# Cross-attention and butterfly FFN on one Trainium2 core: a restaged fold, its first moves on two queues, and token rows transferred row by row

## What is computed

```python
def attn(q, k, v):                    # q = layernorm(x), k = v = context
    kv = k * v                        # along S: r = 0.9 * r + kv
    r = scan(lambda r, t: 0.9 * r + t, kv)
    return q * r
def ffn(x):
    h = x @ W_exp + b_exp             # 512 -> 2048
    h = butterfly(h, up_weights)      # 11 stages of 2x2 pairs
    h = gelu(h + up_bias)
    h = butterfly(h, down_weights)
    return h @ W_con + b_con + down_bias
x = x + attn(layernorm(x), ctx, ctx)
x = x + ffn(layernorm(x))             # x, ctx: 32 x 512 x 512
```

## Time and profile before

| | |
|---|---|
| median of 3 runs | 2850.24 us (2848.72 to 2851.96) |
| the profiled execution: its time | 2851.01 us |
| its span, first to last instruction | 2848.9 us |
| TensorE busy | 2758.7 us, 97% |
| VectorE, ScalarE, GpSimd busy | 2115.7, 1149.7, 546.7 us |
| mean granted TensorE clock | 0.983 of full |
| DMA | 541.31 MB, mean 190 GB/s; SP's queue holds 63.7% of 16 engines' span |

### The profile page before, as it was taken

How to read it: one execution, slowest core, us unless ns; L and a number is a source line. 1 busy time by engine, 2 the same in 40 slices (tenths; PEclk the granted TensorE clock), 3 DMA queues, 4 the chain that set the end, 5 groups by cost and what they waited for, 6 DMA issues and landing times.

```text
span 2848.9 us, 40884 instructions
## 1 busy us (share of the span) xinstructions
PE 2758.7 (97%) x12281; PEld 2277.6 (80%) x12281; DVE 2115.7 (74%) x3500; ACT 1149.7 (40%) x1694; POOL 546.7 (19%) x612
## 2 busy tenths in 40 slices
PE   7859999999999999999999999999999999999999
PEld 6738888888888888888888888888888888888887
DVE  5768778787777878787787878778787877778533
ACT  6554343434334343434334343333434343343432
POOL 4351212112121211212021121201112121112100
PEclk7879999999999999999999999999999999999999
DMA  7597585765758575675758567575856757585543
GB/s 191 121 339 207 161 236 149 215 187 171 223 157 235 152 220 180 178 218 163 226 154 230 168 194 208 170 217 152 247 165 188 206 163 218 155 245 165 171 155 100
DMA packets 296064, 541.31 MB, mean 190 GB/s; under 512 B 38718, under 2 KB 104414, under 8 KB 278902
## 3 DMA queue, kind: packets, MB, share of 16 engines
q1 hardware_dynamic: 290262, 536.90, 63.7%
q10 hardware_dynamic: 4848, 1.13, 0.3%
q0 software_dynamic: 688, 0.17, 0.0%
HBM read 447.89 MB, written 56.62 MB: 177 GB/s over the span
## 4 chain that ended last, share of the span: by engine, by line
PE 93%; SPq 2%; DVE 1%; DMA 1%; issue 1%; ACT 1%; POOL 1%; DVEq 0%; ACTq 0%; POOLq 0%
PE ps L1428 43%; PE ps L1446 24%; PE ps L1459 24%; SPq L458 1%; DVE xop L1056 1%; PE ps L1289 1%; DMA kv<-in_ctx_dram 1%; PE ps L1337 0%; PE ps L1339 0%; PE ps L1328 0%; SPq L422 0%; DMA w_products<-w1r 0%; SPq L428 0%; DMA w_split<-w2s_main 0%; ACT w1r L746 0%
## 5 line engine op out<-in xcount | busy, mean ns | idle before, releaser
L1428 PE MATMUL ps<-xop,w1r 128*128 128x512 f32 x5376 | 1368.7, 390 | 37.6 <-DVE xop L1056 11.9
L1428 PEld LDWEIGHTS ps<-xop,w1r 128*128 128x128 f32 x5376 | 1009.4, 188 | 255.3 <-issue 28.0
L1446 PE MATMUL ps<-w2r,ghi 128*128 128x512 f32 x2048 | 630.7, 389 | 0.0
L1459 PE MATMUL ps<-w2r,ghi 128*128 128x512 f32 x2032 | 625.7, 389 | 0.0
L833 ACT ACTIVATE st<-ps 128x512 f32<-128x512 f32 x384 | 229.4, 597 | 861.8 <-PE ps L1428 861.8
L1134 DVE TENSOR_TENSOR x<-ps,x 128x512 f32<-128x512 f32 x508 | 348.0, 685 | 278.8 <-PE ps L1459 277.9
L1446 PEld LDWEIGHTS ps<-w2r,ghi 128*128 128x128 f32 x2048 | 384.4, 188 | 80.2
L1459 PEld LDWEIGHTS ps<-w2r,ghi 128*128 128x128 f32 x2032 | 381.4, 188 | 79.4
L1157 DVE TENSOR_TENSOR glo<-g,ghi 128x512 fp32r<-128x512 f32 x510 | 381.0, 767 | 86.0 <-ACT ghi L851 85.9
L1152 DVE TENSOR_TENSOR g<-ps,st 128x512 f32<-128x512 f32 x384 | 262.8, 684 | 241.1 <-PE ps L1428 234.5
L837 ACT ACTIVATE g<-g,gelu_bias 128x512 f32<-128x512 f32 x384 | 275.4, 717 | 381.1 <-DVE g L1152 381.1
(11 more groups left out here) (140 smaller groups left out, 1818.1 us busy)
## 6 DMA issues: line engine op xcount, KB each, us to landing
w1r<-w_products SPq DMA_DIRECT2D x889, 256.0 KB, 3.3
w2r<-w_split SPq DMA_DIRECT2D x128, 1024.0 KB, 4.9
x<-in_x_dram SPq DMA_DIRECT2D x128, 256.0 KB, 6.6
raw<-kv SPq DMA_DIRECT2D x512, 64.0 KB, 2.1
out_dram<-x SPq DMA_DIRECT2D x124, 256.0 KB, 3.8
kv<-in_ctx_dram SPq DMA_DIRECT2D x64, 256.0 KB, 6.1
raw<-in_ctx_dram SPq DMA_DIRECT2D x64, 256.0 KB, 4.8
w_split<-w2s_main SPq DMA_DIRECT2D x10, 512.0 KB, 6.0
```

Source lines behind the costliest of these rows:

```text
L1428: last = nc.tensor.matmul(bank[:, :], w1r[:, slot, w, c * P:(c + 1) * P], xop[:, XPOS[m], v, c, :], start=(opens and i == 0), stop=(i == l ...
L1446: last = nc.tensor.matmul(ps_ya[j][:, :], g[:, p % 2, q, j * P:(j + 1) * P], w2r[:, p % 2, kk, w, :], start=(p == 0 and kk == 0 and i == 0 ...
L1459: last = nc.tensor.matmul(ps_yb[:, :], g[:, p % 2, q, j * P:(j + 1) * P], w2r[:, p % 2, kk, w, :], start=(kk == 0 and i == 0), stop=(kk == ...
```

## The change

- **Token rows.** `token_rows` is arranged `t j g i d`; each load and store of a step takes row j of all 128 partitions at once instead of all four rows of 32 partitions. So does the end: the last step's rows go out in four transfers, two on SP and two on ScalarE's queue, instead of sixteen, and the first half's as each is ready.
- **Split parts of the first product** are staged in two spaces by turns: even n in `xop` (positions 4 and 6), odd n in `w1r`, each with its own semaphores; `stmp` gets two sets, so that `weight_sums(n)` waits for n - 2's use.
- **Split parts of the second** go into 10 slots: six lie in blocks of `W1f` that are used up, four in `xop`.
- **Moves.** The first super-block's 32 moves are halved between SP and GpSimd's queue (`first_moves`); both wait for `low_matrix_ready`.
- **Order.** `weight_sums` runs ahead of the bias steps and `token_sums` is cut in two; w_con's upper part is loaded first; `coefs` of the down weights are split earlier; in VectorE's program the scan goes ahead of the statistics, two copies of `high_dn` go to ScalarE, and the first split parts go ahead of the second `normalise`. The copies of `WT` are shared out more evenly.

```diff
-        return a.rearrange("b s d -> (b s) d").rearrange("(g t j i) d -> g t i j d", g=G, t=T, j=J, i=Q)
+        return a.rearrange("b s d -> (b s) d").rearrange("(g t j i) d -> t j g i d", g=G, t=T, j=J, i=Q)
...
             def load_tokens(dst, h, rows, t, loaded):
-                for g in range(G):
-                    sp.dma_start(dst[Q * g:Q * g + Q, J * h:J * h + J, :], rows[g, t]).then_inc(loaded, NX)
+                for j in range(J):
+                    sp.dma_start(dst[:, J * h + j, :], rows[t][j]).then_inc(loaded, NX)
...
-                    for g in range(G):
-                        sp.dma_start(out_rows[g, u * 2 + h], xs[par][Q * g:Q * g + Q, J * h:J * h + J, :])\
-                          .then_inc(out_stored, NX)
+                    for j in range(J):
+                        sp.dma_start(out_rows[u * 2 + h][j], xs[par][:, J * h + j, :]).then_inc(out_stored, NX)
...
+    W2_W1F = {0: 1, 1: 9, 2: 3, 3: 11, 6: 5, 7: 13}
+    W2_XOP = {4: (5, 0), 5: (5, 1), 8: (6, 0), 9: (6, 1)}
+    W2_USE = [(k, 0) for k in range(10)] + [(k, 1) for k in (0, 1, 2, 3, 6, 7)]
...
         def w1_stage(n, g):
             m0, m1 = GROUPS[g]
-            if g == 2 and n % 2 == 0:
-                return xop[:, 4, :, :, :].rearrange("p v c n -> p (v c n)").rearrange("p (m a n) -> p m a n", m=m1 - m0, a=2)
-            return w1r[:, m0:m1, :, :]
+            if n % 2:
+                return w1r[:, m0:m1, :, :]
+            pos, first = ((6, 0), (6, 2), (4, 0))[g]
+            return xop[:, pos, :, :, :].rearrange("p v c n -> p (v c n)").rearrange("p (m a n) -> p m a n", m=4, a=2)\
+                [:, first:first + m1 - m0, :, :]
...
+            def first_moves(h):
+                if h == 0:
+                    pool.wait_ge(low_matrix_ready, 2)
+                pool.wait_ge(xn_turned, (h + 1) * J)
+                move_xT(pool, h, 2, first_moved[h])
+                move_xT(pool, h, 3, first_moved[h])
...
+            for n in range(2, 6):
                 weight_sums(n)
+            token_sums(0, (0, 1), first=True)
+            weight_sums(6)
+            weight_sums(7)
+            token_sums(0, (2, 3), first=True)
```

More of the change, by code:

```diff
@@ L256, in supers @@
             body(U - 1, (U - 1) % 2, first=False, last=True)
-        FOLD = [("WT", k, "dve" if k % 2 and k < KH // 4 else "act") for k in range(KH)]
+        FOLD = [("WT", k, "dve" if k % 2 and not KH // 4 < k < KH // 2 - 1 else "act") for k in range(KH)]
         FOLD += [("low_up", k, "act") for k in range(KH)]
@@ L262, in xattn_ffn_program @@
         FOLD += [("turn_high", q, "act") for q in range(R // 4)]
-        FOLD += [("high_dn", r, "dve" if r % 4 == 3 else "act") for r in range(R)]
+        FOLD += [("high_dn", r, "dve" if r in (3, 7) else "act") for r in range(R)]
         FOLD += [("turn_low", q, "act") for q in range(KH // 4)]
@@ L448, in _ @@
             load_tokens(raw[:, 1, :, :], 0, ctx_rows, 1, ctx_loaded[1])
+            sp.wait_ge(top_picked, 4)
+            load_wcon(1)
             sp.wait_ge(coef_spread, spreads(1, LOWS - 1))
             load_wcon(0)
[L451 to L456, removed]
-                for g in range(G):
[L458 to L464, removed]
             def load_w1(n, slot):
@@ L509, in _ @@
             load_w2(1)
-            for g in range(NG + 1):
-                sp.wait_ge(w1_stored[g], (NP if g < 2 else NP // 2) * NX)
+            for stored in w1_stored[0] + w1_stored[1]:
+                sp.wait_ge(stored, NP // 2 * NX)
             def refill(u, p, m, last):
@@ L685, in _ @@
                 .then_inc(gelu_bias_ready, 1)
-            for n in range(5, NP):
-                weight_sums(n)
-            token_sums(0)
             pool.wait_ge(bias_row_ready, 1)
@@ L893, in _ @@
             supers(act, body)
[L894 to L896 removed]
+            store_last_row(act, 0)
+            store_last_row(act, 2)
         @block.vector
@@ L909, in _, with path_products @@
                 .then_inc(mask_ready, 1)
-            def path_products(dn, first, stages, places, full, spare, outer):
+            def path_products(dn, first, stages, places, full, spare, outer, before_last=None):
                 prev = None
                 for stage in range(stages):
+                    if before_last and stage == stages - 1:
+                        before_last()
                     n = outer << (stage + 1)
@@ L1033, in gate, with normalise @@
                 nc.vector.bn_aggr(mv2[:, j, :], st2[:, j, :]).then_inc(mean2_ready, 1)
-            def normalise(u, h, x, j):
+            def normalise(u, h, x, j, first=False):
                 t = u * 2 + h
@@ L1065, in _ @@
             top_stage(nc.vector, 0).then_inc(low_matrix_ready, 1)
+            for k in range(KH // 4, KH):
+                fold_step("WT", k)
+            coefs_lo(1)
             dve.wait_ge(const_ready, 2)
```

270 lines of the change are left out of this document (150 added, 120 removed).

## The result

The changed kernel takes 3355.73 us, the median of six runs (3350.88 to 3370.40), against 2849.94 for the kernel before: a ratio of 1.178, 95% interval 1.1755 to 1.1801. It is 506 us slower. The profiled execution spans 3356.0 us.

The account below looks back on a forecast made before the run. TensorE, busy 97%, was taken to bound the kernel, behind a fold of small waits. Forecast: 2851 + 795 + 26 + 10 (super-block waits) + 24 (clock) + 23 (end) + 10 (fold) = 3739, so 3740 us, range 3200 to 4050.

Parts of the forecast that it names:

- The outer dimension sets the engines: Token loads and stores: with an outer DRAM dimension of 4, each transfer uses 4 of 16 engines, always the same.
- The price c: Time of one 256 KB token transfer: taken as 3.9 us, between 2.6 (engines at full rate) and 4.7 (w_con's rate).
- the form is that of w_con: Token transfers resemble w_con's load, 112 GB/s over 8 engines or 14.0 each, so 3.9 us lies near that end.
- the sum's own formula: Waiting per middle super-block, from kv's load to w2r's need: 24c - 36.8 us, 56.8 at 3.9, 795 over fourteen.
- TensorE is late once: Per super-block, TensorE waits once, for w2r; delays at earlier gates (x's statistics, a refill) lie inside that wait.
- The clock: After a pause TensorE's matmuls run slower: 1.6 us lost once per super-block, 15 times, 24 us.
- The end: Last stores: eight row transfers in one line end at 2871.7 instead of 2848.9, 23 us lost.
- The fold: Opening up to 215 us: 18 us gained from shorter TensorE waits, 28 lost to late token loads, net +10.
- Costs nothing unless the sums become late: Fold: moving half of the first moves to GpSimd's queue is free unless its sums become late, then at most 13.8 us.
- each at full rate: Rival: token transfers on four engines, each at full rate, 2.6 us per transfer, 3240 us in all; chance 0.14.
- Spread over 16: Rival: token transfers use all 16 engines, no queue forms, the fold's 18 us gain remains, 2833 us; chance 0.09.
- no change: Rival: the fold's gain and loss cancel and the rest is untouched, 2851 us; chance 0.02.

Follow-up runs that it names:

- the dose of 2: Changed kernel with each row transfer issued as two of 64 partitions (outer dimension 2, 128 KB each): 4245.33 us (one run).
- stores alone by rows: Changed kernel with its token loads put back to partition groups, only the stores and the end still row by row: 3010.87 us, ratio 1.0565.

## Why the prediction was right, and where its terms were off

The mechanism was right: few engines, one line on SP's queue, TensorE waiting behind it. The size came from two errors of opposite sign, and the time lies in the range because the range took in the bound of full rate; that much is luck.

- **The outer dimension sets the engines: right.** 4 engines by the share of 0.26, and the dose of 2 fits. They are always the same: with several transfers outstanding, as from 1214 to 1228, others would have raised the share.
- **The price c: mis-sized.** 3.9 us was taken, 2.5 measured. The step that failed is "the form is that of w_con", 14.0 GB/s each as an engine's rate. The row showed a cap on the whole load, divided by the engines that happened to work. The other bound, 2.6 from the full rate, was the value. By the sum's own formula 24 x 2.5 - 36.8 = 23.2 us per super-block; 24.3 of waiting were measured, 364.9 in all where the sum had 831 (795 + 26 + 10). The first super-block's 26 (3.2 at 2.5 us) was 15, the last one's 10 was nothing.
- **"TensorE is late once": wrong, though its price came out nearly right.** It is late three times in a super-block, for two refills and the statistics of x, and in six of the fourteen a fourth time, for the context's square. The formula takes w2r as the gate that ends last, and TensorE waited 5.4 us in all for it: the delays came at the gates before, and w2r's need moved back with them. "Their delays are inside this one" fails for the statistics: the loads of x wait until the stores have landed (SP stood 6.8 us for that before 1241.64), which makes a chain of its own. It costs 11.1 us per super-block with the clock where w2r is never late (stores alone by rows). That the line's 23.2 comes so near the measured 24.3 is thus in part luck.
- **The clock: the mechanism right, the size five times too small.** 24 us for one pause per super-block; three or four pauses cost 8.0 us each super-block, 120 in all. Without this miss in the other direction the total would have been further off: the waits were put 466 us too high, the clock 96 too low.
- **The end:** 23 forecast, 14.6 measured, the same c.
- **The fold:** +10 forecast, +8.2 measured, and not for the reasons given in size. Its gain alone is 9.9 us (first L1498 matmul at 207.06) instead of 18, since the second moves on GpSimd's queue brought the new wait of 12.60 us. "Costs nothing unless the sums become late" was the right condition; they did become late. The late loads cost 18.1 in the changed fold (225.20 against 207.06) instead of 28: the second context's square is at 87.27, 98 was forecast.
- **The rivals.** Of the rivals, "each at full rate" named the right c; its 3240 is 116 us short: the clock's 96, 18 of the fold (-10 against +8.2) and 3 of the end. Its waits, 358 + 5, are the 364.9 measured within 2 us, with the luck just named. Spread over 16 is excluded by the shares, no change by the time.
- **What would show it.** Dips of the clock, waits released by w1r and by VectorE behind L1051, a share near 0.25: all there. Waits for w2r hardly were (5.4 us). "Idle but half as long" was the sign given for a mis-sized c, and it came: some 25 us where 50 were expected. Landings of x and out above 15 us can't be read, since the trace of after gives none for these transfers.

## What to carry to other kernels

Before a DMA's shape is changed, read its outermost dimension on both sides: a tile of 128 partitions against 4 x 32 DRAM rows has the same bytes and count as four transfers of 32 partitions, and worked on four of the 16 engines, while all that was queued behind it on SP waited. When a rate is carried from one transfer to another, ask first whether it is an engine's rate or a cap on that transfer; a share and a rate from one row don't tell, a second row at another number of engines does. And sum a queue's delay once for every chain that hangs on it, write-after-read on a buffer among them, and the clock once for every pause.

## What the runs showed of the hardware that I had not expected

- 16 engines on a load of 16 adjacent partitions with 16 KB rows had a share near 1 and moved 108 to 141 GB/s; a busy share near 1 is not a high rate.
- Four engines on token rows reached 26 GB/s each, two the same 26: few engines ran as fast each as 16 at 405 GB/s (25.3), even with partitions 32 apart.
- Row transfers issued from GpSimd's queue held 0.625 of the 16 engines' time, those from SP's queue 0.26.
- Three or four pauses of 2 to 12 us in some 198 each left the granted clock at 0.50, the lower of its two levels (1.2 GHz), for 3 to 5 us behind them (in the super-block shown 1202 to 1205, 1242 to 1246, 1259 to 1263, 1271 to 1276), and made the same matmuls 4.6% longer (120.1 on 2600.5 us).
